# The queries' and keys' product right behind the turned probabilities, in a vision tower on one core

## What is computed

```python
tokens = einsum('npd,hd->nph', patches, W) + b          # 64 images, 196 patches of 768, D = 192
h = concatenate([cls, tokens], axis=1) + pos_embed       # 64 x 197 tokens
# attention: 12 heads of 16, each query sees 6 keys to either side
qkv = layernorm(h) @ w_qkv
p = softmax(where(valid, q . k_window * 16**-0.5, min))
h = h + (p @ v_window) @ w_proj + b_proj
# experts: top 2 of 8
flat = layernorm(h)
probs = softmax(flat @ router_w.T); top_w, top_i = top_k(probs, 2); top_w /= top_w.sum(-1)
for e in range(8):
    out += sum(top_w * (top_i == e)) * (gelu(flat @ w1[e] + b1[e]) @ w2[e] + b2[e])
h = h + out
```

## Time and profile before

| what | us |
|---|---|
| median of 3 runs | 1504.02 (1502.65 to 1506.02) |
| the profiled execution, its own time | 1507.62 |
| its span | 1505.8 |
| TensorE busy with matmuls | 1400.3 (93%) |
| VectorE busy | 1119.4 (74%) |
| ScalarE busy | 664.8 (44%) |
| GpSimd busy | 913.9 (61%) |

### The profile page before, as it was taken

One profiled execution on the slowest core, in us unless ns is written; L12 is line 12 of the kernel. 1 busy time (PEld: TensorE's weight loads), 2 busy tenths in 40 slices (PEclk: granted clock), 3 DMA queues, 4 the chain that ended last, 5 costly groups with the idle time before them and its releaser, 6 DMA issues.

```text
span 1505.8 us, 50706 instructions
## 1 busy us (share of the span) xinstructions
PE 1400.3 (93%) x17454; PEld 1165.2 (77%) x17455; DVE 1119.4 (74%) x2828; ACT 664.8 (44%) x1148; POOL 913.9 (61%) x902
## 2 busy tenths in 40 slices
PE   5899999999999999999788999999999999999995
PEld 5788788888888888888666677777777777777774
DVE  2578788898888888889677777666666666666663
ACT  2455555554555455455554434333333333333331
POOL 4235666666666667666367866666655666666565
PEclk9999999999999999999899999999999999999998
DMA  5565575767665675755355585555555555554553
GB/s 168 169 195 157 156 195 167 210 168 193 167 196 158 179 202 162 197 165 162 75 99 100 97 142 79 75 75 75 75 72 73 74 74 75 74 74 71 72 73 32
DMA packets 305660, 189.14 MB, mean 126 GB/s; under 512 B 201977, under 2 KB 291397, under 8 KB 304477
## 3 DMA queue, kind: packets, MB, share of 16 engines
q1 hardware_dynamic: 241706, 118.06, 32.2%
q0 software_dynamic: 41680, 41.84, 18.7%
q10 hardware_dynamic: 22115, 27.08, 5.7%
HBM read 89.79 MB, written 65.29 MB: 103 GB/s over the span
## 4 chain that ended last, share of the span: by engine, by line
PE 53%; DVE 23%; issue 8%; POOL 7%; DMA 3%; ACTq 2%; ACT 2%; SPq 1%; DVEq 0%; POOLq 0%
PE scores L1129 7%; PE qk L1146 7%; PE qk L1147 7%; PE qk L1148 7%; PE near L1129 5%; PE mixed L1129 3%; PE token_bank L1129 3%; PE far L1129 3%; PE qk L1251 3%; POOL sorted_scratch L527 3%; DVE st L778 3%; DVE qk L1030 2%; PE near L1182 2%; ACTq L628 2%; POOL payload L539 2%
## 5 line engine op out<-in xcount | busy, mean ns | idle before, releaser
L527 POOL DMA_INDIRECT sorted_scratch<-payload,place x212 | 222.9, 1051 | 56.6 <-issue 56.5
L1182 PE MATMUL near<-we,both_patches 128*120 128x192 f32 x1272 | 225.3, 335 | 18.4 <-DMA both_patches<-in_xt 11.7
L1182 PEld LDWEIGHTS near<-we,both_patches 128*120 128x120 f32 x1272 | 209.5, 186 | 29.1 <-issue 27.3
L512 POOL DMA_INDIRECT out<-both_patches,token x108 | 198.0, 1833 | 36.3 <-issue 36.2
L602 ACT ACTIVATE stage<-near,bias 128x384 f32<-128x384 f32 x103 | 60.0, 582 | 357.2 <-PE near L1129 332.8
L512 POOL DMA_INDIRECT out<-v_side,token x105 | 193.8, 1845 | 36.9 <-issue 36.5
L1146 PE MATMUL qk<-w_hi,stage 128*128 x666 | 164.2, 247 | 1.8 <-DVE v_side L940 1.7
L1146 PE MATMUL qk<-w_hi,both_patches 128*128 x648 | 160.0, 247 | 5.3 <-issue 4.6
L1148 PE MATMUL qk<-w_hi,we 128*128 x666 | 164.2, 246 | 0.0
L1147 PE MATMUL qk<-w_lo,stage 128*128 x666 | 164.2, 246 | 0.0
L1148 PE MATMUL qk<-w_hi,both_patches 128*128 x648 | 159.6, 246 | 0.0
(11 more groups left out here) (271 smaller groups left out, 3605.4 us busy)
## 6 DMA issues: line engine op xcount, KB each, us to landing
both_patches<-in_xt SPq DMA_DIRECT2D x53, 720.0 KB, 4.8
v_diag<-v_scratch SPq DMA_DIRECT2D x159, 89.2 KB
v_scratch<-v_side SPq DMA_DIRECT2D x53, 191.2 KB, 3.8
tabs<-tab_scratch SPq DMA_DIRECT2D x53, 180.0 KB, 4.8
out<-h ACTq DMA_DIRECT2D x52, 180.0 KB
stage<-in_w ACTq DMA_DIRECT2D x8, 1152.0 KB
k_diag<-qk SPq DMA_DIRECT2D x436, 15.8 KB
stage<-in_w ACTq DMA_DIRECT2D x8, 576.0 KB
```

Source lines behind the costliest of these rows:

```text
L512: pool.indirect_dma_start(out=out, out_offset=bass.IndirectOffsetOnAxis(ap=token[k][:, n:n + 1], axis=0), in_=y[k % 2][:, n, :], in_offset ...
L527: pool.indirect_dma_start(out=sorted_dram, out_offset=bass.IndirectOffsetOnAxis(ap=at, axis=0), in_=payload[0:rows, 2 * (block % RING) + n ...
L1182: ins = pe.matmul(near[0:ROWS, n * D:n * D + D], patches[f % 2][:, x, n * ROWS:n * ROWS + ROWS], we[:, x, :], start=(x == 0), stop=(x == K ...
```

## The change

On TensorE, in iterations with t < BLOCKS, the order behind the turned probabilities and the counts becomes: queries' and keys' product, turn of the payload, projection, logits, values. The logits go to the bank `near` in place of `far`, so they wait for `h1_set` of this iteration, and the next embedding waits until they are read (`logit_set`); the projection no longer waits for `logit_set`. The wait for `p_set` before the product of probabilities and values is split in two, one for each half.

On ScalarE, in the same iterations, the high half of queries and keys (`query_key_high`) moves ahead of the payload's features, and the logits' copy stands between the two copies of turned probabilities. In iterations with t >= BLOCKS the order stays, with the logits in `far`. VectorE, GpSimd and SP are not edited.

```diff
 (ScalarE)
+                def logits():
+                    if runs(t, 6):
+                        act.wait_ge(s["routed"], b + 1)
...
+                        act.mul(logit[:, at:at + 2, :], (near if t < BLOCKS else far)[0:ROWS, 0:2 * EXPERTS].rearrange("p (n e) -> p n e", n=2), 1.0 / WS)\
+                           .then_inc(s["logit_set"], 1)
+                def query_key_high():
+                    if runs(t, 1):
+                        act.wait_ge(s["qk_done"], g + 1)
+                        need(act, s["scored"], 2 * (g - 2))
+                        act.copy(qk16[g % QK_RING][:, :, 0, REACH:REACH + SPAN], qk[:, 0:3, 0:SPAN]).then_inc(s["qk_hi_set"], 1)
...
                     if runs(t, 5):
                         attended()
+                    query_key_high()
                     if runs(t, 6):
                         routed_features()
                     if runs(t, 4):
-                        probabilities()
+                        probabilities(0)
+                    logits()
+                    if runs(t, 4):
+                        probabilities(1)
...
 (TensorE)
                     need(pe, s["h1_set"], f)
+                    need(pe, s["logit_set"], t - 6)
                     embed(0)
...
+                if t < BLOCKS:
+                    queries_keys()
+                    turn_routed()
+                    project()
+                    route()
+                    make_values()
+                else:
+                    turn_routed()
+                    queries_keys()
+                    early(3)
+                    route()
+                    make_values()
+                    early(4)
+                    project()
+                    early(5)
                 if runs(t, 4):
-                    pe.wait_ge(s["p_set"], 2 * (c + 1))
                     pe.wait_ge(s["v_in"], VDMA * (c + 1))
                     need(pe, s["norm_done"], c)
                     if counted:
                         pe.wait_ge(s["step"], STEPS * grp + COUNTS_READ)
                     for n in range(2):
+                        pe.wait_ge(s["p_set"], 2 * c + n + 1)
```

More of the change, by code:

```diff
@@ L665, in routed_features, with probabilities @@
                     act.copy(xT2[:].rearrange("p n c r -> p (n c r)"), token_bank[:].bitcast(F16)[:, 0:6 * ROWS]).then_inc(s["xT2_set"], 1)
-                def probabilities():
+                def probabilities(*tiles):
                     need(act, s["pv_done"], c)
-                    for n in range(2):
+                    for n in tiles:
                         act.wait_ge(s["prob_turned"], 2 * c + n + 1)
                         act.copy(pT[:, n].rearrange("p m q -> p (m q)"), scores[0:VKEYS, n, :]).then_inc(s["p_set"], 1)
+                def logits():
+                    if runs(t, 6):
+                        act.wait_ge(s["routed"], b + 1)
+                        if b % 2 == 0:
+                            need(act, s["marks_set"], b // 2)
+                        at = 2 * (b % 2)
+                        act.mul(logit[:, at:at + 2, :], (near if t < BLOCKS else far)[0:ROWS, 0:2 * EXPERTS].rearrange("p (n e) -> p n e", n=2), 1.0 / WS)\
[5 more added lines that the diff above has]
+                        act.copy(qk16[g % QK_RING][:, :, 0, REACH:REACH + SPAN], qk[:, 0:3, 0:SPAN]).then_inc(s["qk_hi_set"], 1)
                 if v < 0:
@@ L702, in body @@
                     if runs(t, 4):
-                        probabilities()
+                        probabilities(0, 1)
                     if runs(t, 6):
@@ L706, in body @@
                     early(3)
[L707 to L714, removed]
+                if t >= BLOCKS:
+                    logits()
+                    query_key_high()
                 if runs(t, 1):
-                    act.wait_ge(s["qk_done"], g + 1)
-                    need(act, s["scored"], 2 * (g - 2))
-                    act.copy(qk16[g % QK_RING][:, :, 0, REACH:REACH + SPAN], qk[:, 0:3, 0:SPAN]).then_inc(s["qk_hi_set"], 1)
                     act.wait_ge(s["v_done"], g + 1)
@@ L1111, in up_chunk @@
                     pe.wait_ge(s["h1_set"], BLOCKS)
+                    pe.wait_ge(s["logit_set"], BLOCKS - 6)
                 elif u < TWO_FROM or (u, m) == (TWO_FROM, 0):
@@ L1233, in body, with turn_routed @@
                     ins.then_inc(s["counted"], 1)
-                if runs(t, 6):
-                    pe.wait_ge(s["lo2"], b + 1)
+                def turn_routed():
+                    if runs(t, 6):
+                        pe.wait_ge(s["lo2"], b + 1)
+                        if runs(t, 1):
+                            pe.wait_ge(s["xT_set"], g + 1)
+                        else:
+                            pe.wait_ge(s["v_set"], BLOCKS)
+                            pe.wait_ge(s["xT2_set"], b)
+                        slot_of = 2 * (b % RING)
+                        turn(payload[:, slot_of:slot_of + 2, :].bitcast(F16), token_bank[:].bitcast(F16), lambda n, c: (3 * n + c) * ROWS)\
+                            .then_inc(s["turned2"], 1)
@@ L1237, in body, with queries_keys @@
+                def queries_keys():
                     if runs(t, 1):
                         pe.wait_ge(s["xT_set"], g + 1)
[L1239 to L1253, removed]
@@ L1254, in body @@
-                early(3)
-                if runs(t, 6):
-                    pe.wait_ge(s["xT2_set"], b + 1)
+                        need(pe, s["qk_main"], g)
+                        for j in range(3):
+                            for i, (x, w, half) in enumerate(PRODUCTS):
+                                ins = pe.matmul(qk[:, j, 0:SPAN], wqk[half][:, w, 128 * j:128 * j + 128], xT1[:, x, :],
+                                                start=(i == 0), stop=(i == len(PRODUCTS) - 1))
+                        ins.then_inc(s["qk_done"], 1)
@@ new lines, in route @@
+                def route():
+                    if runs(t, 6):
+                        pe.wait_ge(s["xT2_set"], b + 1)
+                        if t < BLOCKS:
+                            pe.wait_ge(s["h1_set"], t + 1)
+                        elif runs(t, 5):
+                            pe.wait_ge(s["oT_set"], d + 1)
+                        else:
+                            pe.wait_ge(s["h2_set"], BLOCKS)
+                        for n in range(2):
+                            for j, (x, w, half) in enumerate(PRODUCTS):
+                                ins = pe.matmul((near if t < BLOCKS else far)[0:ROWS, n * EXPERTS:(n + 1) * EXPERTS], xT2[:, n, x, :], wr[half][:, w, :],
+                                                start=(j == 0), stop=(j == len(PRODUCTS) - 1))
+                        ins.then_inc(s["routed"], 1)
@@ new lines, in make_values, with project @@
+                def make_values():
+                    if runs(t, 1):
+                        for n in range(2):
+                            for j, (x, w, half) in enumerate(PRODUCTS):
+                                ins = pe.matmul(token_bank[0:ROWS, n * D:n * D + D], xT1[:, x, n * ROWS:n * ROWS + ROWS], wv[half][:, w, :],
+                                                start=(j == 0), stop=(j == len(PRODUCTS) - 1))
+                        ins.then_inc(s["v_done"], 1)
+                def project():
@@ L1258, in body @@
                     if runs(t, 5):
                         pe.wait_ge(s["oT_set"], d + 1)
[L1260 to L1285, removed]
@@ L1286, in body @@
-                early(5)
+                        if t >= BLOCKS:
+                            pe.wait_ge(s["logit_set"], b + 1)
+                        for n in range(2):
+                            dst = far[0:ROWS, n * D:n * D + D]
+                            pe.matmul(dst, ones16[:, 0:ROWS], bp[:], start=True, stop=False)
+                            for j, (x, w, half) in enumerate(PRODUCTS):
+                                ins = pe.matmul(dst, oT[:, x, n * ROWS:n * ROWS + ROWS], wp[half][:, w, :], start=False, stop=(j == len(PRODUCTS) - 1))
@@ new lines, in project @@
+                        ins.then_inc(s["proj_done"], 1)
+                if t < BLOCKS:
+                    queries_keys()
[3 more added lines that the diff above has]
+                    make_values()
+                else:
+                    turn_routed()
[6 more added lines that the diff above has]
+                    early(5)
```

## The result

The changed kernel took 1524.76 us (median of 4 runs, 1520.15 to 1531.71) against 1505.02 (median of 4, 1502.65 to 1509.55): a ratio of 1.0128, with a 95% interval of 1.0098 to 1.0158. It is slower by 20 us. The profiled execution has a span of 1518.3 us against 1505.8. It is the quickest of the four (1520.15 us), set against a slower one of before (1507.62 us), and shows some 13 of the 20 us.

A forecast was written before the change was run, and what follows sets the result against it. The bound was a loop over two iterations: turned probabilities, logits, VectorE's work, key DMAs, exponentials. Later logits added 16.6 and 5.6 us, 22 in all, to the 1504.0 median, giving 1526, range 1508 to 1536.

The forecast's parts named there:

- Steps 1 and 2: On TensorE, odd iterations' query-key product starts 0.64 us sooner; on ScalarE the logits' copy starts at 408.57, not 407.53.
- Step 3: On VectorE, logits 1.04 us late move the rank step and everything queued behind it, so the following exponentials too.
- Step 4: Delay reaching the end: 16 odd iterations at 1.04 us, where TensorE waits before L1212, and 7 at 0.8: 22 us.
- the sum: The total delay forecast over the 23 odd iterations, 16.6 us plus 5.6 us: 22 us slower.
- main case: The loop's delay with its own bounds, 24 to 32 us, key DMAs perhaps 11 less: 1514 to 1536, chance 0.72.
- Step 5: Edits costed at nothing: TensorE's 0.25 us wait before the logits' product, later probabilities' and values' copies, SP's slip, new waits.
- Rival A: TensorE's payload gap is pure loss and VectorE takes up the later logits: 7.3 us back, 1497, chance 0.07.
- Rivals C and D: Shifted SP issue: ScalarE's key DMAs dearer or patches late, 1542 or 1548 (chance 0.06); or DMAs cheaper, 1513 to 1507 (0.08).
- Rival B: Each delay falls into the other's slack and iterations stay bound by TensorE's own work: no change, 1504, chance 0.07.

## Why the prediction was right

The prediction was 1526 us in a range of 1508 to 1536, slower with 0.84; measured 1524.8.

Steps 1 and 2 hold to a few hundredths in the iteration shown. The product started 1.06 us behind the turned probabilities, as worked out; TensorE's wait came out at 0.2 us (0.25 expected), the logits' copy at 5.03 (4.98 expected: 408.57 less 403.59). As a mean over the odd iterations it moved from 4.01 to 4.92.

Step 3 holds in kind: the rank step in odd iterations waits in all 23 and drags the rest with it, and the kernel with nothing but a late copy of the logits shows it without any change on TensorE. In size VectorE waits 0.87 us more in each odd iteration of the profiled execution, where I had 1.04.

Step 4 had 22 us. The profiled execution shows 14.8 over 22 pairs, 0.67 a pair; the medians show 20. By the medians the size is nearly right, by the profiled executions it is half as large again as the measured one, so that 1526 lies within 2 us of the median is in part luck. The sum had its split from a wrong reading: TensorE stands waiting before L1212 in only 12 of the 23 odd iterations of before (11.6 us), and in 10 even ones (7.8 us), which I had called almost none. What the sum needs is another count, the odd iterations in which the exponentials end less than 0.1 us before they are turned; it is 15, and so near my 16. After the change it is 9: in the 14 others the exponentials are ready before TensorE, and take up part of the delay. TensorE's wait now stands in all 22 even iterations between (0.4 to 2.4 us), as foretold.

What the sum left out stands on VectorE. From its first rank step to its last, over these 22 pairs, it is idle for 23.0 us more (101.1 against 78.1) and busy for 8.7 us less (525.5 against 534.2). The idle time is not the logits' alone: the wait for the embedding (L1002) grew as well, from 6.0 us to the 14.7 shown further up. Its line of before, 100 to 720 us:

```profile
DVE h L987 <- PE near L1182: 6.0, 8, 1.7
```

And the busy time fell because the copy of 24 columns meets GpSimd's L557 less often: 32.4 us before and 23.3 after over the 22 pairs. I had no term for either. The prediction's main case also has a lower end, 1514, that does not follow from its terms: 24 less 11 on 1504 is 1517.

Step 5 holds in what it costed at nothing. The small edits gave 0.9994. The wait before the logits' product, which I had taken for covered in even iterations, may cost something: with the two copies exchanged it is gone, and about 7 us are back, but the logits come only 0.09 us sooner, and the way of the rest is open. Whether such a wait on TensorE costs by itself is not shown; the product moved alone has one of 0.85 us in each iteration together with later logits.

Rival A, that the payload's gap comes back as a gain, fell with the result: the gap is gone, VectorE waits 20.0 us longer for the logits, and the time is 20 us longer. The rule of the Trainium skill, page "Perfetto Trace Analysis", section "Identifying Performance Opportunities", is to look at the gaps of the most contended engine and let what they wait for start sooner; taken to TensorE's gap alone it gave the wrong sign here. But I had picked TensorE by the busy time of its matmuls, which the same section of the Trainium skill calls no good measure; it goes by the busy share of the weight loads, or by the share of peak arithmetic. The weight loads are 520.7 us in the earlier trace rows, under VectorE's 541.7, and so by that measure the rule points to VectorE and its wait for the logits, which the change made longer. Rivals C and D looked to the key DMAs. From the end of the division to the exponentials it is 3.03 us for those of odd and 3.21 for those of even iterations before, as a mean over 23 of each, and 2.99 and 3.23 after; and no wait of TensorE for the patches is among its waits after. The shifted issue on SP shows in neither. Rival B, no change, needed slack in the exponentials; TensorE waited for them in 10 of the 22 even iterations before and in all 22 after.

## What to carry to other kernels

Where two engines are both nearly full, price a new order by the loop that passes through both: find the instruction on the other engine that waits for each moved result, and whether it is waiting already. A result that came later to an engine that already waited for it cost 0.7 to 1.2 us for each us of lateness, by the pairs of the changed kernel (0.67 for 0.91), of the early projection (0.85 for 0.96) and of the late copy (1.3 for 1.1). What came earlier earned nothing here until VectorE's order was changed to use it. Here the change made queries and keys early and the logits late, while VectorE still asked for the logits first; with VectorE's order turned to match, the same change is the fastest kernel. Count also how long the other engine's instructions take where they now fall: a copy that takes 0.17 us alone took up to 0.91 us beside a GpSimd instruction.

## What the runs showed that I had not expected

Moving the rank steps later, in the kernel before, won nothing by itself (ratio 1.0014 where 0.993 was expected). A copy's round trip between two TensorE groups, with nothing placed between them, was 0.85 us of TensorE's waiting in each iteration; with the projection's 1.09 us of matmuls between them it was 0.2 where the high half was copied first, and gone where the payload's features were. VectorE's copy of 24 columns ended with GpSimd's L557 whenever it started beside it, and so a part of VectorE's load hung on when the two met. And the late copy of the logits cost 33 us where 1.1 us in each of 22 loops make 25; the difference stays open. TensorE's mean granted clock was 0.980 to 0.982 in that kernel's six executions, against 0.981 to 0.987 in those with the small edits alone, which may be a part of it; no run tests that.
